# One-column VectorE steps of a four-layer gated network moved to GpSimd, and 127 folded into a guard

## The chip, the cores and the metric

One core of a Trainium2 chip runs the whole program. The metric is the time of one execution in device microseconds, and the figure for the kernel before is the median of three runs. The engines are TensorE (PE, with PEld for its weight loads), VectorE (DVE), ScalarE (ACT), GpSimd (POOL) and SyncE (SP, which starts most transfers). They run side by side, each through its own queue in order, and meet only at semaphores.

## The reference, cut to what matters

The input has 32 samples of 128 tokens by 256 features, with a context of 128 by 192 for each. Four layers follow one another, each a gated cross-attention and then a gated feed-forward. Every one of the eight halves begins with a layer norm over 256 features. The scalars that the change touches are these:

```python
def _layernorm(x, axis=-1, eps=1e-05):
    m = jnp.mean(x, axis=axis, keepdims=True)
    v = jnp.var(x, axis=axis, keepdims=True)
    return (x - m) / jnp.sqrt(v + eps)

def act_quant(x):                      # layer 0, feed-forward: both linear maps
    scale = 127.0 / jnp.clip(jnp.max(jnp.abs(x), axis=-1, keepdims=True), 1e-05)
    return jnp.clip(jnp.round(x * scale), -128, 127) / scale

def moe(x, gate_w, up_w, down_w):      # layer 2, feed-forward: a share per token
    gp = jax.nn.softmax(xf @ gate_w.T, axis=-1)
    ew, _ = jax.lax.top_k(gp, K)       # K = 2
    ew = ew / (jnp.sum(ew, axis=-1, keepdims=True) + 1e-09)
    ef = jax.nn.silu(xf @ up_w.T) @ down_w.T
    out = ef * jnp.sum(ew, axis=-1, keepdims=True)
```

Layer 1 routes each token to one of eight experts, and its output is weighted by the softmax probability of that expert. With the largest logit subtracted, this is one over the sum of the exponentials. The last layer's feed-forward (three blocks of two linear maps with a norm between) is a stage of its own at the end.

## The kernel before, in words

A sample fills the 128 partitions: a partition holds a token. In the first stage (to about 2670 us) four samples are in flight, each in a "lane" with its own buffers and two PSUM banks, and every lane makes eight passes. A lane runs cross-attention L0, the quantized feed-forward ("bit"), cross-attention L1 and routing ("route") for its eight samples, then "mix", L2, "self" (layer 2's small transformer) and L3 for the same eight. The experts' work is done on gathered tiles between these. In the last stage (2687 us to the end) eight lanes make four passes of layer 3's feed-forward.

Each engine's program of a lane is a Python generator that gives up its turn at every `yield`. The order in which an engine takes the lanes' turns is written out by hand as strings of digits in `ORDER`, one for each engine and stage, and `turns` (line 333) replays it. Engines wait for each other through `t.<engine>.at(p, name)`, and `.tell` counts the signals in the order of the `STAGE` table. An engine whose next turn is not ready holds all turns behind it.

A norm is `dve_norm` (line 700): bn_stats (L702), bn_aggr (L704), the addition of epsilon in one column (L706), then, after a yield, `(x - mean) * rstd` over 128 by 256 (L716). Between the two turns GpSimd raises the one column to the power -0.5 (`pool_rstd`, L1399). There are seven norms for each lane and pass in the first stage, 224 in all, and four in the last, 128 in all.

`dve_bitlinear` (line 789) finds the largest magnitude of a row, guards it (L802, L844), inverts it (L803, L845) and multiplies by 127 (L804, L846). `m.deq` (L1057, L1058) holds the weights' scale over 127. `dve_route` ends with the inverse of the sum and its product with the gate (L885, L886). `dve_transformer` turns the eight gate exponentials into a share with max8 and six short instructions (L983 to L989), and the share is read by L1000, behind the down projection. On GpSimd a lane also builds the keys' masked copies (L1414, 128 by 512, for L0, L2, self and L3), scales L1's probabilities (L1439), adds biases (L1426), works the RMS factors (L1447, L1449) and starts the indirect transfers (L1466, L1475, L1488, L1504).

```python
def pool_rstd(pool, m, t, p, l, sub=""):
    pool.wait_ge(*t.dve.at(p, f"{l}.var{sub}"))
    pool.tensor_tensor(t.tiny[:, 1:2], t.tiny[:, 0:1], m.minus_half[:], ALU.pow
                       ).then_inc(*t.pool.tell(p, f"{l}.rstd{sub}"))
```

Of the kernel before, what the change touches and what calls it, by code (L numbers as in the profile page):

```python
# [10 lines left out]
ALU = mybir.AluOpType  # L11
# [4 lines left out]
P = 128  # L16
# [23 lines left out]
NORM = {"pe": "", "dve": "st ag var xn", "act": "", "pool": "rstd"}  # L40
# [13 lines left out]
        "pool": "rstd xb n0 n1 n2 n3",  # L54
# [6 lines left out]
        "pool": "rstd",  # L61
# [3 lines left out]
        "dve": NORM["dve"] + " lg mx sub hot hmx one rcp wt",  # L65
        "act": "xnT ex",
        "pool": "rstd",
# [20 lines left out]
for cross in ("L0", "L2", "L3"):  # L88
    STAGE[cross] = {
        "pe": NARROW["pe"],  # L90
        "dve": NORM["dve"] + " " + narrow_signals(cross) + " x",
        "act": NARROW["act"],
        "pool": "rstd " + NARROW["pool"] + " xb",
    }
STAGE["self"] = {
    "pe": NARROW["pe"].replace("kv xnT q", "xnT k q v") + " unT gate up0 up1 down",
    "dve": NORM["dve"] + " un " + narrow_signals("self") + " u un2 xu gm gs top8 rcp sc add eps rcp2 f sl0 sl1 x",
    "act": "sq " + NARROW["act"].replace("k v xnT q", "xnT k q v") + " sq2 unT gex th0 th1",
    "pool": "rstd ms f1 " + NARROW["pool"] + " ms2 f2",
# [3 lines left out]
    "dve": "cp st ag var h " + " ".join(f"y{b} st{b} ag{b} var{b} xn{b} h{b}" for b in range(BLOCKS)) + " out",  # L103
    "act": " ".join(f"hT{b} gl{b}" for b in range(BLOCKS)),
    "pool": "rstd " + " ".join(f"hb{b} rstd{b}" for b in range(BLOCKS)),
# [47 lines left out]
def sequence_a(n):  # L153

    for half in (FIRST, SECOND):
# [8 lines left out]
        "3032012413442132143243214323412141212231123322122112112213112332312313143342313242314120313302322000"  # L164
        "3003223200120122301200300302013133123010110132221230210220323323202132213212313021023023113313233012"
        "1302101331010010211013203321203110000222100020202032003130210010303233333211122112101230202123202122"
        "3222133031212013021333112033203320313300021031131131101121022330312210020103222020000010030023300012"
        "1133333303201101221121213022222322021022303332321020033030102013231231331330211133131011212131021103"
        "0103002200203002022120103021003032013303032333222121031222232122101230212011331232320010333010030332"
        "1332112031312311303111111211020112001000003323212121232200130030031002101030303033030213113211101230"  # L170
        "2222012230232233231202302210331123231133102231103013302003120211311331102110333201120023000122210010"
        "2020023102203300201011333200333111211331022022203112220322122032103223033322333010301331223001103133"
        "2001132311211033112110113033002000212100030012002101200232020331220023330203033311031222321210122013"
        "1123201122322332020330120002323310033232302313311301211101112011021023110303011012002023002002222000"
        "1211330320010233322332332300012131002031010010011132110323132023122213022121031000010003231323331320"
        "3303222201311013111210112030310332030122032201020311101230132033103230020222132012132211013223313023"
        "3030100233033120123212012231110231103230311003302102232210023001213011331133021302020201232002213221"
        "1011332210333213032330010023320221221101311213011230113033321022302102003001213001133321103220212302"
        "2210302021200131103123330233103330010203222021311012311103203303111002321020232001032313303121011320"
        "1023020120223203122321313013213000102031332021220123101120131021101032032231230320010321301213101332"  # L180
        "3320102003201222302122131031231033000201331202333221201312103111020113100323302321202003012310213011"
        "3313230102002032122203212021131310230003302133021230232312013012103110102030111003032332220213103121"
        "011310230303103222120222312201213102010303013230331320332310101310110103001110030310101010"
    ),
    "pe": (
        "1323232314121333222111332321321213123241142222111133332211222112133122133213134223012301201031200213"
        "1032302030323023020321003002312323120102123013202320112321321321023320130110133322223011303011002120"
        "3133032202211011230230203331230120320120120120320032011300310310230231013212001020121323100122323003"
        "1220321023210323212302131031122122130030311013302031132130212310122033320321101120323020223303201120"
        "2101300132031023120102031023031231002300312321020321001123203123021230103132023123021301301021203322"  # L190
        "0130102323331221303020103321132031021021100320322121331120032023123001303102101201321030020313212300"
        "3232230120001220331032013221310230232013231300220122301313013232331132120302101033133201101202112103"
        "1301102203230211311022300231012031100120312121213323231213232131310010012313003321102013032310322301"
        "2321032302312123310322130220110313030302201111333221031021210203321112120203303302113203203112100303"
        "2200213301201301030212021200300233121312120021212310032103202310120313210232130213202312321301222020"
        "1331031003302301312133320231201303313012112012033120202011331130302032131203020131200120302013020130"
        "1300010322121203031320012301202310320320121230220323130013022303120231320123103302232121313031110221"
        "0103323232002110120230201310101323010231202200211011020320313132211002300123131300232320012021230310"
        "1202103213130202102023202303030231232021203001222331312010230321310230132013211000121221030233113101"
        "3102303103202233231311313122213133221232132130230003101320120123303121101030310223023011231231020321"  # L200
        "1032123021132101330132012023230231003101232120030130131202022102132330302123102121333010213303232010"
        "3213211203103231301010220231132023030031213210212300203123123102013320302031232032131210320131203213"
        "2012132120331021302022103310312310213213130031021100022021320132023312320201120310310312133013132003"
        "2320212111300321030223211032202012033112321321032012102020131210013303213323203010123012031012321323"
        "2301100130313210323221312130102032103012102121230023323201302022011021033032110130213012301302302301"
        "0113223101233000220301102123313213020030310132021012330213110031023203203012023103121232120303131012"
        "3322211313231030201202103010322330201321010323020310113232231012301301320102313202323000122011010123"
        "1110220002112021213001320133020201330120301122230312203231320123121301103123221213210130303212021333"
        "0031023232012012023010303310213212320303110123130210321320323000232103101012133022001012120321121020"
        "1312031323200013301310221330231032201323120212130311302312220332031101201221331300302231302012012010"  # L210
        "3203313103210220332013120101033121302302303021010132231213032200101202132002012131001301230120320313"
        "1132021303230302132032021023120313031020221121033231110010133013210320213031221221031203233102322121"
        "1001201331320020203203032123131131200003113012232002301321020101310310303111303103001331301303103100"
        "111000111001010100"
    ),
    "pool": (
        "3021113331222321221132231100033220323122212313333010111200310202202330000113322110222223311003333312"
        "1111003120022020000331122332101222233001133031033211110032200000212332213013222221103033003333211100"
        "1131122000002123321210000030320001010200200002222331130303331331111121020233300121120000220300313312"
        "0200221212233222201133303111313320332021111103033200012101003200023133000212212122032232030033331121"  # L220
        "1101110130000220002231302233112222220011330033223333022011001100001111233332122212000110300000000000"
# [1057 lines left out]
def act_bitlinear(act, m, t, p, l):  # L1279
# [19 lines left out]
    for half, bank in enumerate((t.a, t.b)):  # L1299
        if half == 0:  # L1300
            act.wait_ge(*t.dve.at(p, f"{l}.rs2"))
# [719 lines left out]
```

## Time and profile before

| | |
|---|---|
| three runs | 2935.18, 2938.9, 2942.4 us, median 2938.9 |
| the profiled execution | 2956.94 us, of which the span from first to last instruction is 2955.7 |
| TensorE | matmuls 90% busy, weight loads 73% |
| VectorE | 75%, 5402 instructions |
| ScalarE | 59% |
| GpSimd | 33%, 1404 instructions |
| DMA | 31 GB/s on average, a share of a few per cent after the first 75 us |
| granted TensorE clock | 0.967 of full speed on average |

The page says first how long each engine was busy. Then it says which chain of work ended last: from the last instruction it goes back at each step to what released it, or to the instruction before it on its engine. A busy share can be high without the engine setting the end, and time on the chain is what a change can shorten. "issue" is time in which an engine waited for nothing the profile shows.

### The profile page before, as it was taken

Reading aid. Unit: us, or ns where it says so; the run is one execution under the profiler, and the core shown is the slowest. Engines: PE = TensorE matmul, PEld = TensorE weight load, DVE = VectorE, ACT = ScalarE, POOL = GpSimd, SP = SyncE. Lnnn points to the kernel's source line nnn. Section 1 sums busy time; section 2 is a strip of 40 time slices with the busy share of each in tenths; the row PEclk is TensorE's granted clock in tenths of the full one; section 3 lists DMA queues with packets and bytes.
Section 4 is the critical chain, followed back from the end, with each engine's and each line's share of the span. In section 5 each row is a group of like instructions: output and inputs, shape, how many; then the busy total and the mean of one; then the engine's idle time right before and its main releaser. Section 6 shows DMA issues by size and latency. Waiting matters only on the chain.

```text
span 2955.7 us, 61780 instructions
## 1 busy us (share of the span) xinstructions
PE 2666.5 (90%) x24164; PEld 2164.5 (73%) x24164; DVE 2224.2 (75%) x5402; ACT 1743.2 (59%) x4657; POOL 980.4 (33%) x1404
## 2 busy tenths in 40 slices
PE   6888999898899989898899999899999998997988
PEld 4767777677677767677677777778777877776766
DVE  7677686868676776867677777778877886867888
ACT  4667667676566666676465555556565655653433
POOL 2222313222433433223533442333322333224545
PEclk8899999999999999999999999999999999998999
DMA  5000000000011211100011221000000001001010
GB/s 179 5 21 11 21 10 19 10 14 17 19 46 51 69 46 37 31 12 26 19 39 57 62 73 35 24 23 17 21 17 16 20 18 30 5 5 33 29 40 19
DMA packets 84091, 92.20 MB, mean 31 GB/s; under 512 B 15252, under 2 KB 77208, under 8 KB 83800
## 3 DMA queue, kind: packets, MB, share of 16 engines
q1 hardware_dynamic: 75352, 59.91, 6.5%
q0 software_dynamic: 8448, 28.34, 3.3%
q8 instruction: 191, 3.13, 0.5%
q14 instruction: 100, 0.82, 0.1%
HBM read 65.36 MB, written 22.85 MB: 30 GB/s over the span
## 4 chain that ended last, share of the span: by engine, by line
PE 53%; DVE 32%; ACT 6%; issue 4%; POOL 3%; DMA 1%; another core or an unknown queue 1%; SPq 0%; DVEq 0%; POOLq 0%; ACTq 0%
PE psum L387 12%; PE psum L363 11%; PE psum L356 9%; PE psum L413 5%; DVE tiny L735 5%; DVE big L743 4%; PE psum L425 3%; PE psum L542 3%; PE psum L380 2%; PE psum L370 2%; PE psum L377 2%; DVE big L822 2%; PE psum L536 2%; DVE xn L716 1%; DVE psum L732 1%
## 5 line engine op out<-in xcount | busy, mean ns | idle before, releaser
L387 PE MATMUL psum<-ident,big 128*128 128x128 f32 x2816 | 423.6, 286 | 75.9 <-ACT big L1221 36.3
L1399 POOL TENSOR_TENSOR tiny<-tiny,minus_half 128x1 f32<-128x1 f32 x224 | 129.7, 579 | 994.8 <-DVE tiny L706 993.9
L1221 ACT ACTIVATE big<-big 128x512 f32<-128x512 f32 x512 | 312.3, 632 | 227.8 <-DVE big L743 226.1
L387 PEld LDWEIGHTS psum<-ident,big 128*128 128x128 f32 x2816 | 324.1, 145 | 145.4 <-ACT big L1221 68.7
L735 DVE TENSOR_REDUCE tiny<-psum 128x8 f32<-128x1024 f32 x256 | 312.8, 1222 | 54.3 <-PE psum L413 49.4
L743 DVE TENSOR_TENSOR big<-psum,tiny 128x512 f32<-128x512 f32 x512 | 330.0, 686 | 8.8
L413 PE MATMUL psum<-head_keys,small 64*128 64x256 f32 x2048 | 284.1, 400 | 23.6 <-ACT big L1228 13.9
L1414 POOL TENSOR_TENSOR head_keys<-big,head_rows 128x512 f32<-128x512 f32 x256 | 265.4, 1056 | 0.0
L413 PEld LDWEIGHTS psum<-head_keys,small 64*128 64x128 f32 x2048 | 183.7, 187 | 77.0 <-issue 56.4
L1439 POOL TENSOR_TENSOR big<-big,tiny 128x512 f32<-128x512 f32 x128 | 137.1, 1073 | 307.9 <-DVE tiny L778 307.5
L1265 ACT ACTIVATE big<-psum,tiny 128x128 f32<-128x128 f32 x512 | 182.1, 384 | 40.2 <-DVE tiny L773 39.9
L387 PE MATMUL psum<-ident,small 128*128 128x128 f32 x896 | 156.7, 284 | 17.4 <-DVE small L751 8.3
L1228 ACT ACTIVATE head_keys<-psum 128x512 f32<-128x512 f32 x256 | 145.9, 600 | 34.8 <-PE psum L387 30.9
L1228 ACT ACTIVATE big<-psum 128x512 f32<-128x512 f32 x256 | 146.8, 601 | 18.7 <-PE psum L387 16.4
L387 PEld LDWEIGHTS psum<-ident,small 128*128 128x128 f32 x896 | 100.9, 142 | 56.1 <-ACT small L1232 15.8
L716 DVE TENSOR_SCALAR xn<-x,mv,tiny 128x256 f32<-128x256 f32 x192 | 108.5, 565 | 43.3 <-POOL tiny L1399 34.9
L542 PE MATMUL psum<-w_L,head_keys 128*128 128x256 f32 x512 | 127.2, 392 | 6.6 <-ACT head_keys L1275 4.4
L356 PE MATMUL psum<-xnT,w_up 128*128 128x128 f32 x1024 | 128.6, 280 | 0.0
L356 PE MATMUL psum<-xnT,w_L 128*128 128x128 f32 x1024 | 127.7, 278 | 0.9 <-ACT xnT L1252 0.8
L356 PEld LDWEIGHTS psum<-xnT,w_up 128*128 128x128 f32 x1024 | 120.8, 194 | 5.1 <-issue 4.6
L356 PEld LDWEIGHTS psum<-xnT,w_L 128*128 128x128 f32 x1024 | 119.8, 192 | 6.2 <-issue 3.2
L1377 ACT ACTIVATE byT<-psum,beta,gamma 128x128 f32<-128x128 f32 x192 | 76.8, 456 | 72.5 <-PE psum L387 72.3
(319 smaller groups left out, 6656.3 us busy)
## 6 DMA issues: line engine op xcount, KB each, us to landing
ctxT<-in_ctxT SPq DMA_DIRECT2D x64, 128.0 KB
after_L_xattn<-x SPq DMA_DIRECT2D x64, 128.0 KB, 1.7
mixture_out<-spare SPq DMA_DIRECT2D x46, 128.0 KB
x_in<-in_x SPq DMA_DIRECT2D x32, 128.0 KB
mixture_in<-xn SPq DMA_DIRECT2D x32, 128.0 KB, 1.7
x_in<-after_L_xattn SPq DMA_DIRECT2D x32, 128.0 KB
bx_in<-after_L_xattn SPq DMA_DIRECT2D x32, 128.0 KB, 2.1
out<-bout SPq DMA_DIRECT2D x32, 128.0 KB, 1.7
```

The costliest lines, as they stand in the source:

```text
L356: last = pe.matmul(bank[:, j * S:(j + 1) * S], wt[:, k, n * P:(n + 1) * P], src[:, k, :], start=k == 0, stop=k == KD - 1)
L363: last = pe.matmul(bank[:, 0:n], srcT[:, k, :], wt[:, k, c0:c0 + n], start=k == 0, stop=k == chunks - 1)
L387: last = pe.transpose(bank[:, k * P:(k + 1) * P], src[:, k * P:(k + 1) * P], identity)
L413: last = pe.matmul(t.ab[:, half, cols], t.qT[rows, r, :], keys[rows, cols], start=True, stop=True)
L542: last = pe.matmul(t.b[:, 0:D], t.kT_wide[:, k, :], m.w["L1o"][:, CH * r + k, :], start=k == 0, stop=k == CH - 1)
L716: dve.tensor_scalar(dst, src, t.mv[:, 0:1], t.tiny[:, 1:2], ALU.subtract, ALU.mult).then_inc(*t.dve.tell(p, f"{l}.{out}{sub}"))
L735: dve.tensor_reduce(top, s8, AX.X, ALU.max).then_inc(*t.dve.tell(p, f"{l}.top{r}"))
L743: dve.tensor_tensor(t.e[half], s8[:, mine, :], top[:, mine].rearrange("p (h o) -> p h o", o=1).to_broadcast([P, CH, S]), ALU.subtract).the ...
L1221: last = act.activation(flat, flat, ACT.Exp, scale=DH ** -0.5)
L1228: act.activation(t.eTs[c].rearrange("p h s -> p (h s)"), t.ab[:, c % 2, :], ACT.Copy).then_inc(*t.act.tell(p, f"{l}.eT{c}"))
L1265: last = act.activation(t.e[half][:, j, :], t.ab[:, half, j * S:(j + 1) * S], ACT.Exp, scale=WIDE ** -0.5, bias=t.tiny[:, 8 + h:9 + h], ac ...
L1414: pool.tensor_tensor(t.head_keys[r], t.kT[:, r:r + 1, :].to_broadcast([P, CH, S]), m.head_rows[:].rearrange("p (h o) -> p h o", o=1).to_br ...
```

## The change

VectorE loses the addition of epsilon in every norm. GpSimd does it ahead of its power, and waits for bn_aggr instead. In the quantized feed-forward the guard's instruction takes a second operation, times 1/127, so the two multiplications by 127 fall away, and the 1/127 leaves `m.deq`. The two instructions of the expert weight become `pool_weight`, a power of -1 and a product on GpSimd, and `dve_mix` waits for it. The six instructions of the gate share become `pool_share`, five instructions on GpSimd that compute (p1 + p2) / (p1 + p2 + 1e-9 * sum), and L1000's instruction waits for it. Signal names follow. All ten `ORDER` strings are different from the first digit on. VectorE's first-stage string goes from 1990 to 1958 turns and GpSimd's from 956 to 1020. Those of the others keep their lengths.

```diff
 def dve_norm(dve, m, t, p, l, src, dst, sub="", out="xn"):
     dve.bn_aggr(t.mv[:], t.stats[:]).then_inc(*t.dve.tell(p, f"{l}.ag{sub}"))
-    dve.wait_ge(*t.dve.at(p, f"{l}.ag{sub}"))
-    dve.tensor_scalar(t.tiny[:, 0:1], t.mv[:, 1:2], LN_EPS, None, ALU.add).then_inc(*t.dve.tell(p, f"{l}.var{sub}"))
     yield
...
-    then(dve.tensor_scalar(mx, mx, 1e-5, None, ALU.max), "mxc")
+    then(dve.tensor_scalar(mx, mx, 1e-5, 1.0 / 127.0, ALU.max, ALU.mult), "mxc")
     then(dve.reciprocal(rs, mx), "rcp")
-    then(dve.tensor_scalar(rs, rs, 127.0, None, ALU.mult), "rs")
...
-    then(dve.tensor_scalar(mx, mx, 2e-5, None, ALU.max), "mx2c")
-    then(dve.reciprocal(rs, mx), "rcp2")
-    dve.tensor_scalar(rs, rs, 127.0, None, ALU.mult).then_inc(*t.dve.tell(p, f"{l}.rs2"))
+    then(dve.tensor_scalar(mx, mx, 2e-5, 1.0 / 127.0, ALU.max, ALU.mult), "mx2c")
+    dve.reciprocal(rs, mx).then_inc(*t.dve.tell(p, f"{l}.rcp2"))
...
 def dve_route(dve, m, t, p, l):
-    dve.wait_ge(*t.act.at(p, f"{l}.ex"))
-    then(dve.reciprocal(sm, sm), "rcp")
-    dve.tensor_scalar(m.weight[:, sample:sample + 1], sm, m.gf["L1"], None, ALU.mult
-                      ).then_inc(*t.dve.tell(p, f"{l}.wt"))
-    yield
...
 def dve_mix(dve, m, t, p, l):
+    dve.wait_ge(*t.pool.at(p, "route.wt"))
...
 def dve_transformer(dve, m, t, p, l):
     dve.max(top, lg).then_inc(*t.dve.tell(p, f"{l}.top8"))
-    then(dve.reciprocal(sm, sm), "rcp")
-    then(dve.tensor_scalar(top[:, 0:2], top[:, 0:2], sm, None, ALU.mult), "sc")
-    then(dve.tensor_tensor(rr, top[:, 0:1], top[:, 1:2], ALU.add), "add")
-    then(dve.tensor_scalar(f1, rr, 1e-9, None, ALU.add), "eps")
-    then(dve.reciprocal(f2, f1), "rcp2")
-    dve.tensor_scalar(f2, f2, rr, None, ALU.mult).then_inc(*t.dve.tell(p, f"{l}.f"))
...
-    dve.wait_ge(*t.dve.at(p, f"{l}.f"))
+    dve.wait_ge(*t.pool.at(p, f"{l}.f"))
...
 def pool_rstd(pool, m, t, p, l, sub=""):
-    pool.wait_ge(*t.dve.at(p, f"{l}.var{sub}"))
+    pool.wait_ge(*t.dve.at(p, f"{l}.ag{sub}"))
+    pool.tensor_scalar(t.tiny[:, 0:1], t.mv[:, 1:2], LN_EPS, None, ALU.add).then_inc(*t.pool.tell(p, f"{l}.var{sub}"))
+    pool.wait_ge(*t.pool.at(p, f"{l}.var{sub}"))
     pool.tensor_tensor(t.tiny[:, 1:2], t.tiny[:, 0:1], m.minus_half[:], ALU.pow
...
+def pool_weight(pool, m, t, p, l):
+    sample, sm = p * LANES_A + t.n, t.tiny[:, 3:4]
+    pool.wait_ge(*t.act.at(p, f"{l}.ex"))
+    pool.tensor_tensor(sm, sm, m.minus_one[:], ALU.pow).then_inc(*t.pool.tell(p, f"{l}.inv"))
+    pool.wait_ge(*t.pool.at(p, f"{l}.inv"))
+    pool.tensor_tensor(m.weight[:, sample:sample + 1], sm, m.gf["L1"], ALU.mult).then_inc(*t.pool.tell(p, f"{l}.wt"))
+    yield
...
+def pool_share(pool, m, t, p, l):
+    sm, rr, f1, f2 = t.tiny[:, 6:7], t.tiny[:, 3:4], t.tiny[:, 4:5], t.tiny[:, 5:6]
+    pool.wait_ge(*t.dve.at(p, f"{l}.top8"))
+    pool.tensor_tensor(rr, t.tiny[:, 16:17], t.tiny[:, 17:18], ALU.add).then_inc(*t.pool.tell(p, f"{l}.two"))
+    pool.tensor_scalar(f1, sm, 1e-9, None, ALU.mult).then_inc(*t.pool.tell(p, f"{l}.eps"))
+    pool.wait_ge(*t.pool.at(p, f"{l}.eps"))
+    pool.tensor_tensor(f1, f1, rr, ALU.add).then_inc(*t.pool.tell(p, f"{l}.sum"))
+    pool.wait_ge(*t.pool.at(p, f"{l}.sum"))
+    pool.tensor_tensor(f2, f1, m.minus_one[:], ALU.pow).then_inc(*t.pool.tell(p, f"{l}.inv"))
+    pool.wait_ge(*t.pool.at(p, f"{l}.inv"))
+    pool.tensor_tensor(f2, f2, rr, ALU.mult).then_inc(*t.pool.tell(p, f"{l}.f"))
+    yield
```

## Rows read from the trace of the kernel before

**Rows 1.** The page's busy time of each engine.

```profile
PE 2666.5 (90%) x24164; PEld 2164.5 (73%) x24164; DVE 2224.2 (75%) x5402; ACT 1743.2 (59%) x4657; POOL 980.4 (33%) x1404
```

**Rows 2.** Busy times by stretch (us and count by engine, then clock, DMA, GB/s).

```profile
100.00:1400.00 1300.00, 1172.82 (x11791) 953.44 (x11791) 937.75 (x2577) 872.41 (x2578) 399.90 (x495) 0.97 0.09 27
1400.00:2600.00 1200.00, 1117.95 (x10179) 918.23 (x10172) 921.59 (x1746) 681.77 (x1613) 406.59 (x613) 0.99 0.10 29
2687.00:2956.00 269.00, 236.76 (x1152) 186.70 (x1152) 233.92 (x767) 109.27 (x289) 144.68 (x224) 0.94 0.09 28
```

**Rows 3.** The page's chain that ended last, by engine.

```profile
PE 53%; DVE 32%; ACT 6%; issue 4%; POOL 3%; DMA 1%; another core or an unknown queue 1%; SPq 0%; DVEq 0%; POOLq 0%; ACTq 0%
```

**Rows 4.** Groups by form on DVE: busy us, mean ns, idle before.

```profile
L716 DVE TENSOR_SCALAR xn<-x,mv,tiny 128x256 f32<-128x256 f32 x192 | 108.5, 565 | 43.3 <-POOL tiny L1399 34.9 <-issue 7.7
...
L706 DVE TENSOR_SCALAR tiny<-mv 128x1 f32<-128x1 f32 x224 | 34.4, 154 | 7.8
...
L706 DVE TENSOR_SCALAR btiny<-bmv 128x1 f32<-128x1 f32 x128 | 19.7, 154 | 4.4
...
L985 DVE TENSOR_SCALAR tiny<-tiny 128x2 f32<-128x2 f32 x32 | 10.2, 320 | 1.1
...
L886 DVE TENSOR_SCALAR mix_weight<-tiny,gates 128x1 f32<-128x1 f32 x32 | 6.9, 214 | 1.1
L989 DVE TENSOR_SCALAR tiny<-tiny 128x1 f32<-128x1 f32 x32 | 6.8, 214 | 1.1
L986 DVE TENSOR_TENSOR tiny<-tiny 128x1 f32<-128x1 f32 x32 | 6.8, 213 | 1.1
...
L988 DVE RECIPROCAL tiny<-tiny 128x1 f32<-128x1 f32 x32 | 5.2, 164 | 1.1
...
L804 DVE TENSOR_SCALAR tiny<-tiny 128x1 f32<-128x1 f32 x32 | 4.9, 154 | 1.1
```

**Rows 5.** The chain at 2237 us: start, us, what.

```profile
2237.60 0.24 DVE tiny L985
2237.84 0.02 issue
...
2238.45 0.21 DVE tiny L989
2238.66 0.59 DVE big L995
```

**Rows 6.** The chain at 490 us, through a norm.

```profile
489.90 0.16 DVE tiny L706
490.07 0.07 issue
490.13 0.56 POOL tiny L1399
```

**Rows 7.** Groups by form on POOL.

```profile
L1399 POOL TENSOR_TENSOR tiny<-tiny,minus_half 128x1 f32<-128x1 f32 x224 | 129.7, 579 | 994.8 <-DVE tiny L706 993.9
...
L1449 POOL TENSOR_TENSOR tiny<-tiny,minus_half 128x1 f32<-128x1 f32 x64 | 35.7, 558 | 5.3
...
L1447 POOL TENSOR_SCALAR tiny<-tiny 128x1 f32<-128x1 f32 x64 | 12.4, 193 | 138.1 <-ACT small L1331 96.1 <-ACT small L1327 40.0
```

**Rows 8.** The timeline at 2237 us: start, us, instruction.

```profile
2237.35 0.16 DVE L983 MAX8 tiny<-tiny 128x8 f32<-128x8 f32 x1
...
2247.21 0.47 DVE L1000 SCALAR_TENSOR_TENSOR x<-psum,tiny,x 128x256 f32<-128x256 f32 x1
```

**Rows 9.** The timeline at 1887 us.

```profile
1886.89 3.83 DVE L716 TENSOR_SCALAR xn<-x,mv,tiny 128x256 f32<-128x256 f32 x1 [1.02 <-POOL tiny L1399]
1887.79 0.13 POOL L1412 MEMSET small<- 128x16 f32 x1
1887.85 2.03 POOL L1414 TENSOR_TENSOR head_keys<-big,head_rows 128x512 f32<-128x512 f32 x2
```

**Rows 10.** The line L716 alone: duration ns min/median/max.

```profile
L716 DVE TENSOR_SCALAR xn<-x,mv,tiny x192: 378/412/3828, 56.8 to 2646.3; 128x256 f32<-128x256 f32 x192
```

**Rows 11.** Who waited for whom: us in total, times, longest us.

```profile
DVE xn L716 <- POOL tiny L1399: 37.0, 59, 1.4
```

More of the change, by code:

```diff
@@ L37 @@
 ENGINES = ("pe", "dve", "act", "pool")
-NORM = {"pe": "", "dve": "st ag var xn", "act": "", "pool": "rstd"}
+NORM = {"pe": "", "dve": "st ag xn", "act": "", "pool": "var rstd"}
 NARROW = {
@@ L53 @@
         "act": "k0 v0 xnT q0 p0 p1 eT0 eT1 oT0 q1 k1 v1 p2 p3 eT2 eT3 oT1",
-        "pool": "rstd xb n0 n1 n2 n3",
+        "pool": NORM["pool"] + " xb n0 n1 n2 n3",
     },
@@ L57 @@
         "pe": "xiT rows h0 h1 aT0 aT1 xT0 xT1 out",
[2 rows of a table removed]
[2 rows of a table added]
         "act": "xiT rows cen0 cen1 th0 th1 rnd0 rnd1 xT0 xT1",
-        "pool": "rstd",
+        "pool": NORM["pool"],
     },
@@ L64 @@
         "pe": "xnT rt",
-        "dve": NORM["dve"] + " lg mx sub hot hmx one rcp wt",
+        "dve": NORM["dve"] + " lg mx sub hot hmx one",
         "act": "xnT ex",
-        "pool": "rstd",
+        "pool": NORM["pool"] + " inv wt",
     },
@@ L92 @@
         "act": NARROW["act"],
-        "pool": "rstd " + NARROW["pool"] + " xb",
+        "pool": NORM["pool"] + " " + NARROW["pool"] + " xb",
     }
@@ L96 @@
     "pe": NARROW["pe"].replace("kv xnT q", "xnT k q v") + " unT gate up0 up1 down",
-    "dve": NORM["dve"] + " un " + narrow_signals("self") + " u un2 xu gm gs top8 rcp sc add eps rcp2 f sl0 sl1 x",
+    "dve": NORM["dve"] + " un " + narrow_signals("self") + " u un2 xu gm gs top8 sl0 sl1 x",
     "act": "sq " + NARROW["act"].replace("k v xnT q", "xnT k q v") + " sq2 unT gex th0 th1",
-    "pool": "rstd ms f1 " + NARROW["pool"] + " ms2 f2",
+    "pool": NORM["pool"] + " ms f1 " + NARROW["pool"] + " ms2 f2 two eps sum inv f",
 }
@@ L102 @@
     "pe": " ".join(f"hT{b} y{b} xT{b} z{b}" for b in range(BLOCKS)),
-    "dve": "cp st ag var h " + " ".join(f"y{b} st{b} ag{b} var{b} xn{b} h{b}" for b in range(BLOCKS)) + " out",
+    "dve": "cp st ag h " + " ".join(f"y{b} st{b} ag{b} xn{b} h{b}" for b in range(BLOCKS)) + " out",
     "act": " ".join(f"hT{b} gl{b}" for b in range(BLOCKS)),
-    "pool": "rstd " + " ".join(f"hb{b} rstd{b}" for b in range(BLOCKS)),
+    "pool": "var rstd " + " ".join(f"hb{b} var{b} rstd{b}" for b in range(BLOCKS)),
 }
@@ L169 @@
[L169 to L178, printed above, removed]
@@ L215 @@
+        "333000333003030300"
     ),
     "pool": (
[L217 to L220, printed above, removed]
@@ L299, in names_of_lane @@
         if tile_of(n, p, l):
-            early = {"pe": ["kv", "kv0"], "act": ["v", "v0"], "dve": ["var"], "pool": []}[engine]
+            early = {"pe": ["kv", "kv0"], "act": ["v", "v0"], "dve": ["ag"], "pool": []}[engine]
             at = max([stage.index(n) + 1 for n in [(p, f"{l}.{e}") for e in early] if n in stage], default=0)
@@ L1056, in dve_constants @@
     then(dve.tensor_scalar(m.absum[:, 0:2], m.setup_bank[:, 0:2], 1.0 / (HID0 * D), 1e-5, ALU.mult, ALU.max), "clip")
-    dve.tensor_scalar(m.deq[:, 0:1], m.absum[:, 0:1], 1.0 / 127.0, None, ALU.mult)
-    dve.tensor_scalar(m.deq[:, 1:2], m.absum[:, 1:2], m.gf["L0"], 0.5 / 127.0, ALU.mult, ALU.mult
+    dve.tensor_copy(m.deq[:, 0:1], m.absum[:, 0:1])
+    dve.tensor_scalar(m.deq[:, 1:2], m.absum[:, 1:2], m.gf["L0"], 0.5, ALU.mult, ALU.mult
                       ).then_inc(*m.s.dve.tell(0, "setup.deq"))
@@ L1518, in pool_lane @@
         yield from pool_rstd(pool, m, t, p, "route")
+        yield from pool_weight(pool, m, t, p, "route")
     yield from pool_mix(pool, m, t, 0)
@@ L1528, in pool_lane @@
         yield from pool_rms(pool, m, t, p, "self", "sq2", "ms2", "f2")
+        yield from pool_share(pool, m, t, p, "self")
         if p == 0:
@@ L1550, in pool_program @@
     pool.memset(m.minus_half[:], -0.5)
+    pool.memset(m.minus_one[:], -1.0)
     pool.memset(m.magic[:, 0:1], MAGIC)
```

206 lines of the change are left out of this document (110 added, 96 removed), and 4 rows, old and new, of the table STAGE.

## The prediction

> **What bounds the kernel now.** I read the busy shares first [rows 1]. TensorE's matmuls fill 90% of the span and VectorE 75%. ScalarE and GpSimd are far below. Then I read the shares by stage [rows 2]. In both halves of the first stage TensorE is ahead (1173 of 1300 us, 1118 of 1200 us), with VectorE at 938 and 922. In the last stage the two are equal (237 and 234 of 269 us), and GpSimd reaches 145. The third view is the chain that ended last [rows 3]: TensorE 53%, VectorE 32%, ScalarE 6%, GpSimd 3%. So the end is set by two engines that hand over to each other. VectorE holds the chain for 0.32 x 2956 = 946 us, which is 43% of its 2224 busy us. A microsecond taken off VectorE is therefore worth less than half a microsecond, and TensorE, idle for only 82 us of the second half's 1200, stands right behind it.
>
> **What leaves VectorE.** 352 additions of epsilon cost 34.4 + 19.7 = 54.1 us. Three instructions of L804's kind (L804, L846, L987) cost 3 x 4.9 = 14.7, three reciprocals at L988's price (L885, L984, L988) 3 x 5.2 = 15.6, and L886, L985, L986 and L989 6.9 + 10.2 + 6.8 + 6.8 = 30.7 [rows 4]. The sum is 115 us in 672 instructions, 5% of VectorE's time. These groups show 1.1 us of idle time for 32, so each instruction also brings some 0.03 us in which the engine waits for its own predecessor [rows 4, 5].
>
> What counts is how much of it lies on the chain. I followed the chain through the whole span and counted the pieces of these lines. In the first stage there are 180 pieces with 28.5 us (69 of them L706, with 10.1 us; nine passes of the share). In the last there are 66 of L706 with 6.8 us. One of each pattern stands here, a share [rows 5] and a norm [rows 6]. Each brings an issue piece of 0.03 us, 5.4 and 2.0 us in all. **Off the chain: 28.5 + 5.4 + 6.8 + 2.0 = 42.7 us.** The guard's second operation I cost at nothing, since L804's 154 ns is the price of a one-column operation with a constant and the engine's fixed part makes all of it. The bounds are 0 and 0.06 us (L886's 214 ns, whose factor comes from memory) for 64 instructions, at most 4 us. The two edits of `m.deq` happen once.
>
> **What the norm gains in length.** On that path [rows 6] the power follows L706 after 0.07 us. Afterwards GpSimd adds epsilon itself. The nearest row is L1447, the same kind of instruction, at 193 ns, and the power behind it (L1449) waits 5.3 / 64 = 0.083 us [rows 7]. So the addition costs 0.276 us ahead of a power. L706 and its gap cost 0.19, so a norm takes 0.09 us longer from bn_aggr to rstd. VectorE waited for the power 59 times in the form most used [rows 11]. The chain runs through 33 powers (29 in the first stage, 4 in the last), so **33 x 0.276 = 9.1 us come back** (8.0 and 1.1).
>
> **What GpSimd takes over.** 352 additions at 0.193 are 68 us. The weight is a power (0.579) and a product. The share is one tensor-scalar (0.193), one power (0.558) and three tensor-tensors. The trace has no short tensor-tensor on GpSimd but the power, so I bound one by 0.193 and 0.558 [rows 7] and take the middle, 0.38, since it reads two operands like the power but does less with them. The sum is 68 + 32 x 0.96 + 32 x 1.89 = 159 us (135 to 182), and about 290 waits for its own predecessor at 0.083 add 24 us. That makes 183 us on an engine that is busy 33%. The share hides behind the up and down projections: GpSimd needs 32 times some 2.2 us, while from max8 to L1000 there are 9.9 us [rows 8] and at least 6.6 us in the 32 passes. Without that cover each pass would wait 2.2 us, 70 us in all. The new wait of `dve_mix` is for a value worked out long before the lane's second half. Behind it stand VectorE's other turns, and it costs nothing. Both new blocks sit in GpSimd's queue in front of the next norm's addition, of key copies (L1414) and of indirect transfers. They wait for an exponential or for max8, and meanwhile hold those.
>
> **The shared memory port.** L716 lasts 412 ns in the median and up to 3828 [rows 10]. One of the longest, 3.83 us, ends only when GpSimd's run of key copies has ended [rows 9]. Over its 192 instances this is 108.5 - 192 x 0.412 = 29 us [rows 4, 10]. Over all of VectorE's lines the excess over each line's median is 97 us, beside some 842 us of GpSimd tensor work, or 0.115 us for each. With 159 us more on GpSimd that is 18 us on VectorE, 43% of it on the chain, so 8 us. But a one-column instruction makes a much shorter block than a run of two key copies, and L985, whose mean of 320 against 0.24 us on the chain [rows 4, 5] shows that it was caught too, leaves. I take **4 us** (3.5 and 0.5), with bounds 0 and 8.
>
> The Trainium skill ("SBUF — State Buffer", Who interferes with whom) says that VectorE and GpSimd share one port pair as an exclusive lock: a VectorE instruction in a two-port mode, or with two inputs in SBUF, and a GpSimd instruction that reads block each other for the whole instruction. The trace agrees [rows 9]. The skill ("Perfetto Trace Analysis", Optimizing Scalar/DVE Operations) adds that offloading between the two might not help, which speaks against this change.
>
> **The sum.** On the chain the first stage loses 28.5 + 5.4 - 8.0 - 3.5 = 22.4 us and the last 6.8 + 2.0 - 1.1 - 0.5 = 7.2 us. Of the first I keep half. When VectorE's pieces shrink the next to be late is TensorE, already busy 93% in the second half and 90% in the first [rows 2], so I take the middle between all and nothing, 11.2 us. The last stage I keep whole, because there VectorE is as full as TensorE and eight lanes keep work ready. Together this is 18.4 us. The profiled execution took 2956.9 us and would take 2938.5. It lies 18 us above the median of 2938.9, and from that median the forecast is **2920.5 us**, 0.6% less.
>
> **The order.** All ten strings are new. Turns per lane advance about alike in old and new, with the lanes renamed, so I put the mean effect at zero. Its bound is TensorE's idle time in the first stage, 127 + 82 = 209 us [rows 2]. An order that wins or loses a fifth of it moves 40 us. This is the largest unknown.
>
> **The rivals.** (a) *More than the chain's half.* If all 29.6 us are kept and the order gains a little beside, the time is 2938.9 - 30 to - 60, say 2900. VectorE's 32% of the chain speaks for it, TensorE's 93% against. (b) *TensorE takes over.* The relief on VectorE only becomes idle time there, and the first stage yields nothing. With the last stage's 7 us the time is 2932. For it speaks that TensorE is the fuller engine [rows 2]. (c) *GpSimd's queue becomes the wait*, and the kernel is slower. The 183 us are in-order work in front of powers, key copies and L1439. They outweigh the 42.7 us as soon as more than 42.7 / 183 = 23% of them lie on the chain. Today GpSimd is on it with 3% of 2956 = 89 us of 980, or 9%, which speaks against. The 64 new points where it holds other lanes' steps speak for. At 35% it is 64 - 43 = 21 us, so 2960. (d) *The port decides.* If each added GpSimd microsecond blocked VectorE for as long, 159 x 0.43 = 68 us would join the chain: 2938.9 - 43 + 9 + 68 = 2973. This is the skill's lock at its worst. The measured rate of 0.115 speaks against it. (e) That the change does not do what it says would show in the instruction counts. With 115 us taken from the lines named I give it nothing.
>
> **How the numbers follow.** Forecast 0.42 (2908 to 2930), (a) 0.13, (b) 0.20, (c) 0.21 and (d) 0.04. A measurement of this kernel tells about 0.3% from no change, 8.8 us. Faster by more: 0.42 + 0.13 = 0.55. Within: 0.20. Slower: 0.21 + 0.04 = 0.25. The range takes in the whole of (b), most of (a) and the milder half of (c): 2888 to 2955.
>
> **What would show it.** VectorE has about 672 fewer instructions and busy time near 2110 us, and GpSimd 576 more and 1140 us. The addition on GpSimd takes near 0.19 us and a short tensor-tensor between 0.19 and 0.56. VectorE's waits for powers rise from 37 us by some 5. L1000 never waits for GpSimd. TensorE's idle time shrinks by about the gain. The prediction is wrong if VectorE's or TensorE's waits for GpSimd lines grow by tens of us, if long L716 become more frequent, or if a stage changes by more than the chain's pieces allow, which would be the order's doing.

## The result and the profile after

The changed kernel takes 2893.91 us in the median, beside 2937.04 for the kernel before, a ratio of 0.9853 (95% interval 0.9837 to 0.9869). That is 43 us less, where 18 us had been forecast. The direction was right and the size was not. The profiled execution of before lay 20 us above its own median, and that of after on its median, so the two spans (2955.7 and 2891.7 us) overstate the gain. Only the medians are used for it. The granted TensorE clock is 0.967 of full speed in both profiled executions, so the clock is not the cause.

The page of the changed kernel gives busy times, and the chain that ended last:

```profile
PE 2653.2 (92%) x24164; PEld 2160.0 (75%) x24164; DVE 2139.4 (74%) x4730; ACT 1739.2 (60%) x4657; POOL 1139.4 (39%) x1981
...
PE 64%; DVE 22%; ACT 6%; POOL 4%; issue 3%; DMA 1%; SPq 0%; DVEq 0%; POOLq 0%; ACTq 0%
```

VectorE has 672 instructions fewer and 85 us less busy time (115 were summed up, but neighbours overlap). GpSimd has 577 more and 159 us more, both beside [rows 1]. (The overlap shows in dummy_on_vector below: 352 instructions of 0.144 us, 51 us in all, add 17 us of busy time.) On the chain VectorE fell from 32% to 22% and TensorE rose from 53% to 64% [rows 3]. The same stretches as in [rows 2], with the last stage at its new place:

```profile
100.00:1400.00 1300.00, 1195.10 (x12039) 971.81 (x12037) 929.98 (x2379) 883.01 (x2610) 470.12 (x711) 0.97 0.09 27
1400.00:2600.00 1200.00, 1140.61 (x10406) 942.92 (x10406) 896.20 (x1503) 697.56 (x1652) 474.08 (x858) 0.99 0.10 29
...
2627.00:2892.00 265.00, 233.53 (x1152) 184.57 (x1152) 222.63 (x640) 109.97 (x289) 175.04 (x352) 0.95 0.09 29
```

TensorE does more in the same time: 1195 of 1300 us against 1173, and 12039 matmul instructions against 11791. The last stage is 265 us against 269. The gain lies in the first stage. Part of the 22 us in each half comes from the long execution of before that was profiled, and not from the change. eps_on_gpsimd (below) takes the same time as before, and its profiled execution lies on its median. Its two stretches have 3 and 9 us more matmul time than [rows 2], so the changed kernel is ahead of it by 19 and 14 us:

```profile
100.00:1400.00 1300.00, 1175.67 (x11849) 957.28 (x11848) 924.88 (x2457) 872.86 (x2581) 432.92 (x622) 0.97 0.09 27
1400.00:2600.00 1200.00, 1127.05 (x10268) 928.53 (x10267) 919.90 (x1683) 690.25 (x1627) 430.94 (x702) 0.99 0.10 29
```

GpSimd's groups by form show the prices that the prediction could only bound [rows 7]:

```profile
L1388 POOL TENSOR_TENSOR tiny<-tiny,minus_half 128x1 f32<-128x1 f32 x224 | 129.4, 578 | 18.6
...
L1386 POOL TENSOR_SCALAR tiny<-mv 128x1 f32<-128x1 f32 x224 | 54.0, 241 | 635.8 <-DVE mv L705 633.3
...
L1446 POOL TENSOR_TENSOR tiny<-tiny,minus_one 128x1 f32<-128x1 f32 x32 | 18.2, 568 | 65.5 <-ACT tiny L1306 65.4
...
L1456 POOL TENSOR_TENSOR tiny<-tiny 128x1 f32<-128x1 f32 x32 | 6.6, 205 | 113.1 <-DVE tiny L976 113.0
```

The addition of epsilon takes 241 ns there, and 18.6 / 224 = 0.083 us more pass before the power. A short tensor-tensor takes 0.19 to 0.21 us, not 0.38. In the form most used VectorE waited for the power 72 times with 60.5 us, where the prediction expected some 42. Who waited for GpSimd, to be held against [rows 11]:

```profile
DVE xn L715 <- POOL tiny L1388: 60.5, 72, 1.9
```

### The profile page after: what moved, and what is told of

Same layout as the page of the kernel before. It is cut to its first block, busy times and chain, and to the rows that moved or that the text cites. A ratio compares the mean times of both kernels' runs of the same rounds, so it can differ in the third digit from the quotient of the medians.

```text
span 2891.7 us, 61717 instructions
## 1 busy us (share of the span) xinstructions
PE 2653.2 (92%) x24164; PEld 2160.0 (75%) x24164; DVE 2139.4 (74%) x4730; ACT 1739.2 (60%) x4657; POOL 1139.4 (39%) x1981
## 4 chain that ended last, share of the span: by engine, by line
PE 64%; DVE 22%; ACT 6%; POOL 4%; issue 3%; DMA 1%; SPq 0%; DVEq 0%; POOLq 0%; ACTq 0%
PE psum L388 15%; PE psum L364 14%; PE psum L357 10%; PE psum L414 7%; PE psum L426 4%; PE psum L381 3%; PE psum L543 3%; PE psum L371 3%; DVE tiny L734 3%; PE psum L378 2%; DVE big L742 2%; DVE big L820 2%; PE psum L537 2%; DVE xn L715 2%; DVE big L824 1%
## 5 line engine op out<-in xcount | busy, mean ns | idle before, releaser
L388 PE MATMUL psum<-ident,big 128*128 128x128 f32 x2816 | 411.1, 283 | 62.3 <-ACT big L1208 32.1
L1386 POOL TENSOR_SCALAR tiny<-mv 128x1 f32<-128x1 f32 x224 | 54.0, 241 | 635.8 <-DVE mv L705 633.3
L715 DVE TENSOR_SCALAR xn<-x,mv,tiny 128x256 f32<-128x256 f32 x192 | 117.4, 612 | 56.6 <-POOL tiny L1388 55.9
L1388 POOL TENSOR_TENSOR tiny<-tiny,minus_half 128x1 f32<-128x1 f32 x224 | 129.4, 578 | 18.6
```

The source lines that it names most:

```text
L388: last = pe.transpose(bank[:, k * P:(k + 1) * P], src[:, k * P:(k + 1) * P], identity)
L715: dve.tensor_scalar(dst, src, t.mv[:, 0:1], t.tiny[:, 1:2], ALU.subtract, ALU.mult).then_inc(*t.dve.tell(p, f"{l}.{out}{sub}"))
```

## The experiments

Ratios are to the kernel before on the same chip. One chip was 0.8% slower than the rest (before takes 2961 us there), so microseconds are compared only within a set of runs. The four runs measured on it are edits_gathers_first, new_share_on_vector, new_127_unfolded and new_weight_on_vector. Their chains, and that of before in [rows 3], run through "another core or an unknown queue", and those of all other runs do not. So the trace of before seems to be of that chip or of its like, which would explain its 20 us.

### The edits without the order, and the order without the edits

All edits under the old strings:

```diff
 ORDER = {   # the strings of the kernel before
-    dve: 1990 turns, 32 of them the weight's
+    dve: 1958 turns
-    pool: 956 turns
+    pool: 1020 turns, the 64 new ones where their inputs come ready
```

> All edits of the change, but the order strings of the kernel before, with VectorE's 32 dropped turns struck out and GpSimd's 64 new turns put in where their inputs come ready (four of GpSimd's gathers move back behind a weight turn). Theory A, the edits did it and my discount by half was wrong: 2937 - 43 = 2894, at least 30 us faster than before. Theory B, my sum was right and the new order brought the rest: 2937 - 18 = 2919, between 10 and 25 us faster. Were the edits worth nothing, 2937.

It measured 1.0058 (1.0043 to 1.0073), slower than before. The opposite (code of before, strings of after, the turns exchanged the other way):

> The code of the kernel before with the changed kernel's order strings, GpSimd's 64 new turns struck out and VectorE's 32 turns of the weight put in where their input comes ready. Theory A (edits): 2937, within 8 us. Theory B (order): 2937 - 25 = 2912, some 15 to 30 us faster. If the new order only suits the new code, it is slower than 2937.

0.9988 (0.9977 to 1.0). Neither theory fits. The order alone is worth 0.12%, the edits alone cost 0.58%, and together they give 1.5%.

### Where the old order loses

Share and weight moved alone, under the same adapted order:

> The kernel before with the gate share and the expert weight moved to GpSimd, epsilon and 127 as before, and the old order with the 64 GpSimd turns put in where their inputs come ready. All edits under this order took 2951, 13 us more than before, and epsilon's move alone 0. If these two blocks are what holds GpSimd's queue: 2950 or more. If they are hidden behind the projections as I took them to be: 2938 - 13 = 2925, what their 13 us of VectorE pieces on the chain are worth.

1.0030 (1.0018 to 1.0041), slower like the whole change under this order. The first output of "self" (L1000 in before) comes 128 us after the first mix, against 112 before. GpSimd's timeline in that run shows why (L1448 is the weight's power, L1520 the gather of the mixed rows):

```profile
1359.33 0.55 POOL L1390 TENSOR_TENSOR tiny<-tiny,minus_half 128x1 f32<-128x1 f32 x1
1368.35 0.55 POOL L1448 TENSOR_TENSOR tiny<-tiny,minus_one 128x1 f32<-128x1 f32 x1 [8.47 <-ACT tiny L1310]
1368.98 0.19 POOL L1450 TENSOR_TENSOR mix_weight<-tiny,gates 128x1 f32<-128x1 f32 x1
1369.75 1.04 POOL L1520 DMA_INDIRECT yg<-mixture_out,token_place  x1 [0.59 <-issue]
```

The waits between 1290 and 1420 us have the other end of it:

```profile
DVE x L946 <- DMA yg<-mixture_out,token_place: 12.5, 3, 4.3
...
POOL tiny L1448 <- ACT tiny L1310: 10.3, 3, 8.5
```

GpSimd holds a gather behind an exponential that comes late, and VectorE waits for the gathered rows. To take that away, all edits again, with the last weight behind the gather (and GpSimd's string changed in that one stretch to match):

```diff
-        yield from pool_weight(pool, m, t, p, "route")
+        if p + 1 < PASSES_A:
+            yield from pool_weight(pool, m, t, p, "route")
     yield from pool_mix(pool, m, t, 0)
+    yield from pool_weight(pool, m, t, PASSES_A - 1, "route")
```

> All edits under the old order, as new_edits_old_order (2951), but in a lane's last pass the weight's turn stands behind the first gather, so that GpSimd's old turns keep exactly their old order. In share_weight_old_order GpSimd waited 8.5 us for an exponential at 1368 us in front of a gather, VectorE 12.5 us for gathered rows, and the stretch between the first mix and the first output of self took 128 us against 112 before. Theory E (that place cost the edits about 15 us): 2951 - 15 = 2936, level with before. My sum would want 2919. If the loss is spread over the queue, 2951 stays.

0.9955 (0.9937 to 0.9973). With every old turn of GpSimd in its old place the edits are worth 0.45%, 13 us. That one place costs 1.0%, some 30 us, twice what was expected. The stretch from the first mix to the first output of "self" went from 127 us in new_edits_old_order to 113, so 14 of the 30 us are found there, and where the others come from is open. The same code under the new order gives 0.9853.

### Epsilon

```diff
-    dve.tensor_scalar(t.tiny[:, 0:1], t.mv[:, 1:2], LN_EPS, None, ALU.add)
+    pool.tensor_scalar(t.tiny[:, 0:1], t.mv[:, 1:2], LN_EPS, None, ALU.add)   # eps_on_gpsimd
+    # (neither: GpSimd takes the power of mv itself)                          # no_eps
```

> Only the epsilon of the norms goes to GpSimd, 352 instructions of 154 ns off VectorE, under unchanged order strings. My sum for this part on the chain: 16.9 us of L706 and 4 of issue pieces less, 9 us of longer norm and some 3 of port stalls more, so -9, halved in the first stage to -6. Theory A: 9 to 15 us faster. Theory B: 4 to 8 us faster. If GpSimd's longer step before every power decides, no gain.

> Leaves out the addition of epsilon altogether: GpSimd takes the power of the variance itself behind bn_aggr, order strings unchanged. VectorE's relief without GpSimd's price. Beside eps_on_gpsimd it gives the price of the 0.276 us on GpSimd. Theory A (time on VectorE's chain counts in full): 21 us faster or more. Theory B (half of it): 11 to 14 us faster. The difference to eps_on_gpsimd should be 9 to 12 us by my sum.

Moved: 1.0002 (0.9993 to 1.0011). Left out: 0.9904 (0.9885 to 0.9924). So GpSimd's step costs the 31 us that are gained when nobody adds epsilon, three times the 9 to 12 us that were expected. The waits of eps_on_gpsimd, and the chain at one of its norms:

```profile
DVE xn L714 <- POOL tiny L1399: 79.6, 85, 8.1
```

```profile
490.42 0.19 DVE mv L704
490.61 0.08 issue
490.69 0.23 POOL tiny L1397
490.92 0.07 issue
490.99 0.58 POOL tiny L1399
```

The longest of these waits, 8.1 us, has a sibling of 7.7 us in no_eps. Counted over the span, the chain ran through 33 powers in before. In eps_on_gpsimd it runs through 85 (and through 34 in no_eps). In the form most used, VectorE waits for the power 85 times with 79.6 us there and 62 times with 50.2 us in no_eps. These 29 us are nearly as much as the two times differ. The same two cuts under the new order:

> The changed kernel and its order strings, but epsilon goes back to VectorE as before. Under the old order moving it brought nothing (0.02%), leaving it out 31 us, so GpSimd's step cost as much as VectorE's relief. Theory C, the new order hides GpSimd's step: here the kernel is slower than the changed one (2894) by 20 us or more, near 2915 or above. Theory D, the move is worth nothing in any order and the rest of the change with its own order brings the 43 us: 2894 within 8 us.

> The changed kernel and its order strings without any addition of epsilon (left out altogether). What GpSimd's step still costs under the new order. Theory C (hidden): 2894 down to 2885, under 10 us. Theory D (not hidden): as under the old order 31 us less, near 2863.

Back on VectorE: 0.9859 (0.9842 to 0.9875), level with the changed kernel. Left out: 0.9751 (0.9733 to 0.9770), 1.0% or 30 us less than the changed kernel. The new order doesn't hide GpSimd's step either. With the rest of the change in place, epsilon's move gives nothing. Two runs below show that it does give something while other steps are still on VectorE: 0.24% with all three of them there (0.9988 to 0.9964), 0.38% with the share there (0.9922 to 0.9884).

### What a microsecond is worth, engine by engine

Four kernels add one one-column instruction to each of the 352 norms of the kernel before: on VectorE behind the addition with nothing waiting, the same with a wait for its end, on GpSimd behind the power, and on GpSimd in front of it.

```diff
     dve.tensor_scalar(t.tiny[:, 0:1], t.mv[:, 1:2], LN_EPS, None, ALU.add)...
+    dve.wait_ge(*t.dve.at(p, f"{l}.var{sub}"))                    # chained one only
+    dve.tensor_scalar(spare, m.minus_half[:], LN_EPS, None, ALU.add)
+    dve.wait_ge(*t.dve.at(p, f"{l}.dup{sub}"))                    # chained one only
```

> The kernel before with one more one-column instruction on VectorE in each of the 352 norms, behind the addition of epsilon, which nothing waits for. VectorE's queue gets longer, the norm's path to the power does not. Leaving the addition out gave 31 us, more than my 21 from the chain. Theory G (occupancy of VectorE counts): 352 x 0.15 = 54 us x 43% = 23 us slower, ratio 1.008. Theory H (the norm's path counts, not the engine): within 8 us of before.

> As dummy_on_vector, but the extra instruction waits for the addition and the engine waits for the extra one's end, so that all of its 0.19 us is VectorE's (the first dummy ran into its neighbours: busy time rose by 17 us only). 352 x 0.19 = 67 us of queue, path from bn_aggr to the power unchanged. Theory G (VectorE's time counts 43%): 29 us slower, ratio 1.010. Theory H (the path counts, not the engine): within 8 us.

> The kernel before with one more one-column instruction on GpSimd behind each of the 352 powers, with a wait for its own end, which no other engine waits for: 0.276 us of queue each, 97 us, and the path from bn_aggr to the power's end unchanged. Epsilon's step in front of the power cost 28 to 31 us. Theory G' (GpSimd's queue is what costs): 20 to 30 us slower. Theory H (the norm's path): within 8 us of before.

> The kernel before, epsilon still on VectorE, with an extra one-column addition on GpSimd in front of each power, and a wait for it: 0.3 us more from bn_aggr to the power's end in 352 norms, no relief on VectorE. The same instruction behind the power cost nothing (0.9979). Theory H (the path): 28 to 31 us slower, as between no_eps and eps_on_gpsimd, ratio 1.010. My sum for it was 33 x 0.276 = 9 us and halved, 5: ratio 1.002.

| run | ratio (95%) | us |
|---|---|---|
| dummy_on_vector | 1.0019 (1.0007 to 1.0031) | +6 |
| dummy_chained_on_vector | 1.0209 (1.0192 to 1.0226) | +60 |
| dummy_on_gpsimd | 0.9979 (0.9969 to 0.9989) | -6 |
| dummy_before_power | 1.0077 (1.0060 to 1.0094) | +22 |

The busy times and the chain of dummy_chained_on_vector, then the busy times of dummy_on_gpsimd:

```profile
PE 2682.8 (90%) x24164; PEld 2168.6 (72%) x24164; DVE 2292.1 (77%) x5754; ACT 1745.9 (58%) x4657; POOL 970.4 (32%) x1404
...
PE 45%; DVE 41%; ACT 6%; issue 5%; POOL 3%; DMA 1%; SPq 0%; DVEq 0%; POOLq 0%; ACTq 0%
```

```profile
PE 2660.7 (91%) x24164; PEld 2164.9 (74%) x24164; DVE 2210.2 (75%) x5402; ACT 1744.4 (59%) x4657; POOL 1060.3 (36%) x1756
```

The chained dummy adds 68 us to VectorE's busy time [rows 1] and 60 us to the kernel. But busy time is not the time for which it holds the queue. Here is a norm in before, in dummy_chained_on_vector and in dummy_on_vector:

```profile
339.72 0.15 DVE L706 TENSOR_SCALAR tiny<-mv 128x1 f32<-128x1 f32 x1
339.79 1.22 DVE L735 TENSOR_REDUCE tiny<-psum 128x8 f32<-128x1024 f32 x1
```

```profile
347.18 0.15 DVE L706 TENSOR_SCALAR tiny<-mv 128x1 f32<-128x1 f32 x1
347.37 0.15 DVE L709 TENSOR_SCALAR tiny<-minus_half 128x1 f32<-128x1 f32 x1
347.56 1.23 DVE L740 TENSOR_REDUCE tiny<-psum 128x8 f32<-128x1024 f32 x1
```

```profile
343.36 0.15 DVE L706 TENSOR_SCALAR tiny<-mv 128x1 f32<-128x1 f32 x1
343.43 0.14 DVE L708 TENSOR_SCALAR tiny<-minus_half 128x1 f32<-128x1 f32 x1
343.49 1.21 DVE L737 TENSOR_REDUCE tiny<-psum 128x8 f32<-128x1024 f32 x1
```

From L706's start to the next instruction that waits for nothing there are 0.07 us in before and 0.38 in the chained run (medians of 269 and 276 norms). So the chained dummy holds the queue for 0.31 us and not 0.19: it waits for the addition, and what follows waits for it. That is an estimate of 352 x 0.31 = 109 us, of which 60 reach the end, or 55%. The chain moves onto VectorE (32% to 41%). The unchained dummy holds the queue for 0.06 us, 21 us in all, and 6 of them reach the end. On GpSimd the same kind of instruction is free behind the power (80 busy us more, and the kernel even 6 us faster) and costs 22 us in front of it. What counts on GpSimd is the path that others wait on, not its load, as far as 80 us of it show. Theory H, that the norm's path alone decides, fell with the chained dummy, which leaves that path as it was and costs 60 us.

### The parts under the new order

127 alone under the old order, and each part undone under the new one. new_weight_on_vector exchanges 32 turns, new_share_on_vector strikes out 32 of GpSimd's, and new_127_unfolded changes none.

```diff
 # fold_127_alone, on the kernel before; new_127_unfolded is its reverse on the changed one
-    then(dve.reciprocal(rs, mx), "rcp"); then(dve.tensor_scalar(rs, rs, 127.0, None, ALU.mult), "rs")
+    then(dve.reciprocal(rs, mx), "rcp")                 # the guard carries 1/127
 # new_share_on_vector
-        yield from pool_share(pool, m, t, p, "self")
+    then(dve.reciprocal(sm, sm), "rcp") ... dve.tensor_scalar(f2, f2, rr, None, ALU.mult)
 # new_weight_on_vector
-        yield from pool_weight(pool, m, t, p, "route")
+    then(dve.reciprocal(sm, sm), "rcp"); dve.tensor_scalar(m.weight[...], sm, m.gf["L1"], None, ALU.mult)
```

new_share_eps_on_vector puts epsilon back on VectorE as well, and new_order_eps_on_gpsimd is old_code_new_order with epsilon's step on GpSimd.

> The kernel before with 127 folded into the guard alone, 64 instructions of 154 ns off VectorE, order strings unchanged. On the chain before these had 5.2 us in 33 pieces and 1 us of issue. Full worth: 6 us faster (0.2%); halved: 3 us. If replaying an order made for other durations costs by itself: nothing, or slower.

> The changed kernel and its order strings with the two multiplications by 127 back (64 instructions of 154 ns on VectorE). fold_127_alone gave 2 to 4 us under the old order. The same here: 2896 to 2900. If the new order has used up all slack around them: up to 2905.

> The changed kernel, its order strings without GpSimd's 32 share turns, and the six instructions of the share back on VectorE. What the share's move is worth under the new order. VectorE's pieces of the share on the chain before: 10.2 us with their issue time 11.8. Theory F (the share's move is the part that the new order needs): 2894 + 12 or more, 2906 to 2920. If the order alone did it: 2894 within 8.

> The changed kernel with the expert weight back on VectorE, GpSimd's 32 weight turns struck out and VectorE's 32 put in where their input comes ready. On the chain before these had 3.0 us and 0.7 of issue. By that 2894 + 4 = 2898. If the sum of the parts is to make 43 us (order alone 4, epsilon 4, 127 4, share 12), some 15 us are left for the weight: 2909.

> The changed kernel and its order strings with both share and epsilon back on VectorE. One by one they cost 0.31% and 0.06% (in ratios to before, 0.9884 and 0.9859 against 0.9853). If parts add: 0.989. If VectorE's load passes a point where the new order stops working, more: 0.992 or above.

> old_code_new_order (0.9988) with epsilon moved to GpSimd: share, weight and 127 stay on VectorE. If parts add: 0.9982. If the moves help each other under the new order: 0.994 or below.

| run | ratio (95%) | against 0.9853 |
|---|---|---|
| new_127_unfolded | 0.9855 (0.9838 to 0.9871) | +0.02% |
| new_eps_on_vector | 0.9859 (0.9842 to 0.9875) | +0.06% |
| new_weight_on_vector | 0.9864 (0.9848 to 0.9880) | +0.11% |
| new_share_on_vector | 0.9884 (0.9868 to 0.9901) | +0.31% |
| new_share_eps_on_vector | 0.9922 (0.9900 to 0.9943) | +0.69% |
| new_order_eps_on_gpsimd (the other three on VectorE) | 0.9964 (0.9951 to 0.9977) | +1.11% |
| old_code_new_order (all four) | 0.9988 (0.9977 to 1.0) | +1.35% |

fold_127_alone gave 0.9993 (0.9982 to 1.0003), no difference that can be told. The four single parts sum to 0.50%, all of them together to 1.35%. Share and epsilon together cost 0.69%, nearly twice their sum of 0.37%. With intervals of some 0.16% on either side, the first three rows can't be told from nothing. That 0.69% is more than 0.37% is not clear of noise either, but 1.35% against 0.50% is. Under this order the parts help each other. That one part put back is taken up by slack and the next finds none is how I read it, and no run shows it.

## Why the prediction was right or wrong

**What bounds the kernel: right.** TensorE's share of the chain rose to 64% as VectorE's fell, and the gain is TensorE's idle time: against eps_on_gpsimd, which takes as long as before, 33 us more matmul time in the two halves of the first stage.

**VectorE's relief: instructions and rate about right, the part on epsilon too small.** The 672 instructions went. "A microsecond taken off VectorE is therefore worth less than half a microsecond" came out about so: leaving out epsilon took 352 x 0.19 = 67 us off the queue and gave 31 (no_eps), 46%, and that run shortens the norm's path as well. Added, a microsecond of queue is worth 55% (dummy_chained_on_vector). But the sum went by the chain's own pieces of L706 with their issue time, 21 us, and then halved most of it, where 31 came. The chain that ended last shows one path. A likely reason is that cutting a piece also shortens the paths beside it, which no run tests.

**The norm's longer path: mis-sized two- to threefold.** The sum had 33 x 0.276 = 9.1 us and the runs show 22 (dummy_before_power) to 31 (eps_on_gpsimd against no_eps). In the changed kernel VectorE's waits for the power rose by 23.5 us and not by some 5, which is one of the signs of being wrong that the prediction named. The instruction took 0.24 instead of 0.19 us. The greater error was the 33, since the chain then runs through 85 powers. The two errors on epsilon had opposite signs and cancelled in part: with the halving, the relief of some 15 us was 31, and the price of some 5 was 31 too. So the part came out at 0 where the sum had some -6, and that this is close is luck.

**The second operation of the guard, and the cover of the share: right.** The guard's instruction takes 154 ns with its second operation, as without it. L987's instruction (L1000 before) never waits for GpSimd. The only wait in front of it is for the down projection:

```profile
  PE psum L364: 26.5, 15
```

**GpSimd's load and the port: harmless, as taken.** Its 159 us match the 159 of the sum, though by luck, through two errors (0.24 for the addition, 0.19 to 0.21 for the short tensor-tensors). The "about 290 waits for its own predecessor" are 480 by the edits (352 + 32 + 96) and have 42 us in the trace, not 24. It changes only rival (c)'s share. VectorE's excess over its lines' medians went from 97 to 108 us, so 11 where 18 was the ceiling. The 4 us that I took for it on the chain were not measured by themselves. The L716 of [rows 9] ends at 1890.72, which is 0.84 us after the last key copy and not with it. GpSimd's bias addition came in between, here in before:

```profile
1889.85 0.71 POOL L1426 TENSOR_TENSOR x<-x,out_bias_L 128x256 f32<-128x256 f32 x1
```

The Trainium skill's lock ("SBUF — State Buffer", Who interferes with whom) fits that, but 80 added us of one-column work on GpSimd behind the power made nothing slower. Rival (d) falls.

**Rival (a), "say 2900": its number, not its reason.** The measured 2894 lies in its 2879 to 2909, which had a chance of 0.13. It wanted all 29.6 us kept and a small gain of the order beside. The runs show 13 us for the edits and 4 for the order, each alone, so the hit is luck.

**Rival (c), GpSimd's queue: right in mechanism, under the old order.** The weight's turn holds a gather for 8.5 us, and the edits come out 0.58% slower than before. The new strings mostly avoid it: VectorE waits for gathered rows once, 4.9 us, against four times and 16.3 us in new_edits_old_order.

**Rival (b) and the half: near for the edits alone.** The edits under the old order with that place mended give 0.45%, 13 us. The forecast of 18 us was in truth a forecast of this, and the errors on epsilon that cancel helped it there.

**The order: the step that failed.** "I put the mean effect at zero." That is right for the old code (0.12%) and wrong for the new, where it is worth 0.9955 against 0.9853, or 1.0%. I had set a bound of 40 us on it and then left it out of the forecast, as a term that adds to the rest by itself. It doesn't add: order alone 0.12%, edits alone 0.45% at best, both 1.5%. The prediction's last sign, a stage that changes by more than the chain's pieces allow, came true for the first stage.

I take it that an order replayed from a string is fitted to the instruction lengths it was made for. Under the old strings the new code loses at one known place (new_edits_old_order). The old order was adapted in only two ways. A third might bring more, so the 1.0% is the new order's lead over the better of them and no property of the old order. Against edits_gathers_first the changed kernel's VectorE waits less in some places and longer in others. Here edits_gathers_first first, then the changed kernel:

```profile
DVE xn L715 <- POOL tiny L1388: 81.5, 85, 8.1
DVE tiny L748 <- PE psum L388: 68.9, 39, 5.3
DVE x L760 <- PE psum L364: 59.8, 39, 4.1
DVE tiny L777 <- ACT big L1252: 51.6, 32, 5.3
DVE tiny L734 <- PE psum L414: 49.1, 35, 9.6
```

```profile
DVE tiny L748 <- PE psum L388: 88.4, 48, 9.0
DVE tiny L734 <- PE psum L414: 72.8, 50, 6.3
DVE xn L715 <- POOL tiny L1388: 60.5, 72, 1.9
...
DVE x L760 <- PE psum L364: 35.1, 28, 3.0
...
DVE tiny L777 <- ACT big L1252: 26.2, 24, 2.5
```

Three waits shrink by 71 us together and two waits for TensorE's results grow by 43. edits_gathers_first ran on the slower chip, but new_edits_old_order, which did not, shows the same pattern (84.6, 68.1, 59.6, 53.8, 48.2 us).

Which turns of the strings bring this is open. The lanes are numbered otherwise in the new strings, and putting a part of the new order into the old one wasn't tried.

## What to carry to other kernels

Where an edit comes with a new static order, the two are one change: price the order at the new lengths, and give it a term, not only a bound. In these runs short work on the idle engine was free behind what others wait for, and in front of it cost as much as the busy engine gained. The chain's count of pieces is no bound for a lengthening, because the chain moves there (33 powers became 85). And when a kernel is loaded on purpose, count the time for which an instruction holds its queue, from start to next start, and not its busy time.

## What was not expected of the hardware

A one-column tensor-tensor on GpSimd takes 0.19 to 0.21 us and a power of one column 0.57, so the power and not the two inputs makes the length. A one-column tensor-scalar with one operation takes 0.23 to 0.26 us there (L1386 0.241, and 0.257 in the last stage; L1457 0.242; the dummy behind the power 0.230), and the one with two operations (L1447 in before, a multiplication and an addition) 0.19. Why the second operation doesn't lengthen it is open. On VectorE a one-column instruction that nothing waits for holds the queue for 0.06 us, and one chained by waits on both sides for 0.31. An extra instruction on GpSimd behind each power made the kernel 0.2% faster (0.9969 to 0.9989). Why is open.
